# Attention steps of a one-core block laid out anew: values product behind two more products, output parts later, VectorE additions behind the maximum

## What is computed

```
h = rmsnorm(layernorm(x)) * ln_weight
q, k, v = h @ w_q.T, ctx @ w_k.T, ctx @ w_v.T          # 512 -> 32 heads x 128
p = softmax(where(mask, q @ k.T + position_bias, -inf))
x = x + layernorm(x) + (p @ v) @ w_out.T
```

## Time and profile before

| | us |
|---|---|
| runs | 1034.56, 1049.08, 1047.72 |
| median of the runs | 1047.72 |
| the profiled execution | 1043.91 |
| its span, first to last instruction | 1041.8 |

### The profile page before, as it was taken

The page is one execution under the profiler, slowest core; times in us unless marked ns, Lnnn a source line. Parts: engine busy times, 40 slices in busy tenths (PEclk is TensorE's granted clock), DMA queues, the critical chain, the costliest instruction groups (busy, mean ns, idle before and its releaser), DMA issues.

```text
span 1041.8 us, 17308 instructions
## 1 busy us (share of the span) xinstructions
PE 936.6 (90%) x5261; PEld 792.8 (76%) x5261; DVE 721.3 (69%) x1289; ACT 606.9 (58%) x1847; POOL 523.3 (50%) x582
## 2 busy tenths in 40 slices
PE   9989999998988898979898898888897988889998
PEld 8778888886877777867787687777786777668885
DVE  5676965756677586757675667668675868747787
ACT  5777665555656456655564556646565555534564
POOL 2541634574546454654555454645475452204477
PEclk9999999999999999999999999999999999989999
DMA  9223448535565275635672556437562555230101
GB/s 331 68 88 120 162 163 302 206 115 212 184 239 178 95 263 182 236 121 201 206 267 85 212 194 236 149 115 263 179 232 108 204 185 177 88 112 0 32 21 61
DMA packets 61291, 171.70 MB, mean 165 GB/s; under 512 B 6055, under 2 KB 8491, under 8 KB 60988
## 3 DMA queue, kind: packets, MB, share of 16 engines
q1 hardware_dynamic: 61244, 171.11, 47.2%
HBM read 159.56 MB, written 11.53 MB: 164 GB/s over the span
## 4 chain that ended last, share of the span: by engine, by line
PE 53%; DVE 19%; ACT 11%; issue 11%; POOL 4%; DVEq 1%; DMA 1%; SPq 0%; ACTq 0%; POOLq 0%
PE ps_k L363 4%; ACT probs_t L799 4%; PE ps_k L364 4%; PE ps_k L365 4%; PE ps_s L2175 4%; ACT scores L787 4%; PE ps_t L2196 4%; PE ps_o L363 4%; PE ps_q L363 3%; DVE scores L1608 3%; PE ps_q L365 3%; PE ps_v L363 3%; PE ps_q L364 3%; PE ps_v L365 3%; PE ps_v L364 3%
## 5 line engine op out<-in xcount | busy, mean ns | idle before, releaser
L799 ACT COPY probs_t<-scores 32x128 f32<-32x128 f32 x768 | 227.4, 296 | 143.3 <-DVE scores L1612 134.2
L363 PE MATMUL ps_o<-wo_hi,att_hi 128*128 128x512 f32 x256 | 109.0, 426 | 72.5 <-DVE acc L1485 51.8
L787 ACT ACTIVATE scores<-scores,neg_max 128x128 f32<-128x128 f32 x256 | 99.7, 391 | 53.2 <-DVE neg_max L1599 53.0
L363 PEld LDWEIGHTS ps_o<-wo_hi,att_hi 128*128 128x128 f32 x256 | 48.8, 190 | 101.0 <-DVE acc L1485 51.1
L1485 DVE TENSOR_TENSOR acc<-ps_o,acc 128x512 f32<-128x512 f32 x128 | 85.9, 671 | 57.0 <-PE ps_o L365 57.0
L781 ACT CAST att_hi<-ps_t 128x512 fp32r<-128x512 f32 x64 | 37.5, 587 | 146.7 <-PE ps_t L2196 146.6
L1160 POOL TENSOR_TENSOR wq_lo<-raw_q,wq_hi 128x256 fp32r<-128x256 f32 x65 | 47.8, 735 | 125.5 <-ACT wq_hi L620 125.5
L364 PE MATMUL ps_o<-wo_lo,att_hi 128*128 128x512 f32 x256 | 101.9, 398 | 0.0
L365 PE MATMUL ps_o<-wo_hi,att_lo 128*128 128x512 f32 x256 | 101.5, 397 | 0.0
L1119 POOL TENSOR_TENSOR shift<-bias_sb,mask_sb 128x512 f32<-128x512 f32 x64 | 84.5, 1323 | 1.5 <-DVE scores L1595 1.5
L363 PE MATMUL ps_v<-wv_hi,ct_hi 128*128 128x256 f32 x264 | 74.8, 283 | 1.5 <-DVE vv L1439 1.5
(11 more groups left out here) (394 smaller groups left out, 2824.7 us busy)
## 6 DMA issues: line engine op xcount, KB each, us to landing
ring_hi<-scratch_x_t SPq DMA_DIRECT2D x39, 512.0 KB, 4.0
ring_lo<-scratch_x_t SPq DMA_DIRECT2D x39, 512.0 KB, 4.9
ring_hi<-scratch_c_t SPq DMA_DIRECT2D x39, 512.0 KB, 4.2
ring_lo<-scratch_c_t SPq DMA_DIRECT2D x39, 512.0 KB, 5.2
raw_o<-in_w_o SPq DMA_DIRECT2D x16, 512.0 KB, 3.7
raw_q<-in_w_q SPq DMA_DIRECT2D x15, 512.0 KB, 6.1
raw_k<-in_w_k SPq DMA_DIRECT2D x15, 512.0 KB, 7.0
xt_hi<-scratch_x_t SPq DMA_DIRECT2D x13, 512.0 KB, 8.2
```

The costliest lines, as they stand in the source:

```text
L363: pe.matmul(dst, hi_l, hi_r, start=first, stop=False)
L787: e = act.activation(probs[n][:, m, :], scores[n][:, m, :], ACT.Exp, bias=neg_max[:, n, m:m + 1], accum_out=row_sum[:, n, m:m + 1])
L799: last = act.copy(block_of(probs_t, j, i), block_of(scores[n], i, j))
```

## The change

The work is the same; the order on PE, DVE and ACT is another. POOL's and SP's lists are not touched. On PE the values product of a step no longer follows the scores at once but comes behind two (in steps 0 and 4 three) more products, each output part comes about one product later, and the v products and k products around them are dealt out anew; `v_p4` gets a wait for its operand block. On DVE the second residual addition of a step moves into the next step, behind its maximum, together with sums of projections, and the transposes become a function of their own (`turn_blocks`), in steps 3 and 7 behind further additions. On ACT the exponentials come ahead of `attention_high`.

```diff
 # ACT, step
-                attention_high(s - 1)
                 if c % 4 == 2 and more:
                     k_first(G)
+                exponentials(s, n)
+                if c == 4 and coming:
+                    v_first(i + 1, 0)
+                if c % 4 == 1 and more:
+                    q_first(G)
+                attention_high(s - 1)
                 if c % 4 == 3 and more:
                     high_fourth(G)
-                exponentials(s, n)
...
 # DVE, step
                 softmax_front(s, n)
-                attention_rest(s - 1)
+
+                if c == 0 and own:
+                    v_u3(i, 1)
+                if c == 1 and own:
+                    v_c22(i, 1)
+                    v_u4(i, 1)
...
+                add_output(s - 2, (c - 2) % LOOP_STEPS, (1,))
...
+                if c == 3 and own:
+                    v_c21(i, 0)
                 if last and c == 5:
                     q_c12(g)
+                attention_rest(s - 1)
+
+                if c == 7:
+                    k_c11(G)
+                if c == 3:
+                    q_c21(G)
                 softmax_back(s, n)
-                add_output(s - 1, (c - 1) % LOOP_STEPS, (0,))
+                if c % 4 == 3:
+                    add_output(s - 1, (c - 1) % LOOP_STEPS, (0,))
+                    if c == 7:
+                        k_u3(G)
+                        q_c21(G)
+                    k_c21(G)
+                turn_blocks(s, n)
                 if c == 0 and own:
                     v_c22(i, 0)
                     v_u4(i, 0)
...
+                if c % 4 != 3:
+                    add_output(s - 1, (c - 1) % LOOP_STEPS, (0,))
...
-                add_output(s - 1, (c - 1) % LOOP_STEPS, (1,))
...
 # PE, step
                 step_scores(s, c)
+
+                if c % 4 == 0:
+                    q_p5(g)
+                    k_p5(g)
+                if c == 0:
+                    q_p3(g)
+                if c == 4 and coming:
+                    v_p1(i + 1, 0)
+                if c % 4 == 1 and more:
+                    q_p1(G)
+                    q_p6(G)
...
+                if c % 4 == 3:
+                    q_p4(G)
+
                 if c == 0:
                     step_values(s - 1, 7, v_count(i - 1, 14))
...
+                if c == 0:
+                    v_p5(i, 0)
                     k_p3(g)
...
+                    k_p4(G)
                 if c == 4:
                     if coming:
                         v_p1(i + 1, 1)
+                        q_p3(g)
...
+                if c == 7:
+                    k_p2(G)
+                output(s - 1, (c - 1) % LOOP_STEPS, g if c % 4 == 1 else None, (0,))
+
+                if c == 0:
+                    v_p5(i, 1)
+                if c % 4 == 1 and more:
+                    k_p6(G)
...
+                if c == 5 and coming:
+                    v_p6(i + 1, 0)
+                if c == 6:
+                    v_p7(i + 1, 0)
+                if c == 7:
+                    k_p4(G)
...
+                output(s - 1, (c - 1) % LOOP_STEPS, None, (1,))
```

More of the change, by code:

```diff
@@ L857, in step @@
                 if c == 4 and coming:
-                    v_first(i + 1, 0)
                     high_v2(i + 1)
+                    v_first(i + 1, 1)
                 if c % 4 == 0 and more:
                     high_first(G)
-                if c % 4 == 1 and more:
-                    q_first(G)
                 if c % 4 == 2 and more:
@@ L930, in _ @@
             wq1_high_part(3)
-            attention_high(STEPS - 3)
             def mm_high(m):
@@ L1680, in step @@
                 coming = not last
[L1681 to L1688, removed]
+                if c % 4 == 1 and summed and not (last and c == 5):
+                    q_c12(g)
+                if c == 3:
+                    k_c11(G)
+                if c == 6 and coming:
+                    v_u2(i + 1, 0)
+                if c == 7 and coming:
+                    v_u3(i + 1, 0)
+                softmax_front(s, n)
+                if c == 0 and own:
[3 more added lines that the diff above has]
+                    v_u4(i, 1)
                 if c == 4 and not last:
@@ L1706, in step @@
                     q_u4(g)
+                if c % 4 == 1 and summed and not (last and c == 5):
+                    k_c12(g)
+                if c % 4 == 2:
+                    k_u2(G)
+                if c == 6 and coming:
+                    v_u2(i + 1, 1)
                 if c % 4 == 3:
                     q_u3(G)
+                if c == 3:
                     k_u3(G)
[L1710 to L1714, removed]
                 if not own:
@@ L1735, in step @@
                         v_evac(14, 3, 0, done=13)
+                if c % 4 == 2:
+                    q_c11(G)
                 if c == 2 and own:
                     v_c12(i, 1)
-                if c == 3 and own:
-                    v_c21(i, 0)
                 if last and c == 4:
                     v_c21(i, 1)
[L1742 to L1747, removed]
                 if c % 4 == 0 and summed:
@@ L1750, in step @@
                     k_u4(g)
+                if c % 4 == 1 and more:
+                    q_u2(G)
                 if isinstance(i, int) and s == FIRST:
                     block_low(1, wide[0], 7)
[L1753 to L1760, removed]
-                add_output(s - 1, (c - 1) % LOOP_STEPS, (1,))
                 if last and c == 5:
-                    wq1_rest(2)
+                    k_c12(g)
+                    for m in range(3):
+                        wq1_rest(m)
             def target_experts():
@@ L2405, in step @@
                 step_scores(s, c)
+                if c % 4 == 0:
[8 more added lines that the diff above has]
+                    q_p6(G)
+                if last and c == 5:
+                    q_p3(g)
+                if c == 6:
+                    v_p6(i + 1, 1)
+                if c % 4 == 2:
+                    q_p7(G)
+                if c == 2:
+                    q_p2(G)
+                if c == 7:
+                    v_p7(i + 1, 1)
+                if c % 4 == 3:
+                    q_p4(G)
                 if c == 0:
@@ L2498, in step @@
                     v_p4(i, 1)
+                if c == 4 and coming:
+                    v_p2(i + 1, 0)
+                    k_p3(g)
+                if c == 5 and coming:
+                    v_p6(i + 1, 0)
+                if c == 6:
+                    v_p7(i + 1, 0)
+                if c == 7:
+                    k_p4(G)
+                if last and c == 5:
+                    pe.wait_ge(v_out, v_count(i, 14))
+                    for _ in range(4):
+                        pe.matmul(ps_v[:, 0:P], ones[:], ones[:], start=True, stop=True)
+                output(s - 1, (c - 1) % LOOP_STEPS, None, (1,))
+                if c == 1 and not own:
+                    step_v(15, 13, PLAIN)
             for c in range(1, LOOP_STEPS):
```

126 lines of the change are left out of this document (40 added, 86 removed).

## The result

The changed kernel takes 1109.44 us in the median (1109.07 to 1109.97), the kernel before 1047.97: a ratio of 1.062 (95% interval 1.055 to 1.069). The profiled execution's span grew from 1041.8 to 1107.7 us. So it is slower, as forecast, but by 61 us where 25 were forecast, and above the range of 1036 to 1100. (The kernel before has one run more here than in the table of its runs.)

The account below looks back on a forecast made before the run. PE sets the pace, so its waits count. From the profiled 1043.9 us: six turns of +3.45 (+20.7), steps ahead -3, clock +13 less 2, making 1073; range 1036 to 1100, likeliest case 1056 to 1090.

Parts of the forecast that it names:

- forecast, without the clock: Lengths of steps 0 to 7 of the new turn, summing to 115.8 us, +3.45 a turn, before any clock loss.
- The waits for weights: PE waits of 4 to 5 us for `wv_lo` once each in steps 3, 5 and 6, some 80 us or more.
- the third that was named: Over the whole span, PE's waits for `acc` and `att_lo` were to shrink to a third.
- The meetings of DVE and POOL: DVE operations held up by POOL, each meeting costing a whole POOL instruction: 1.1 us in step 6, 1.7 in step 5.
- I take one fall in two: Half of 18 PE waits bring the clock to half, 1.46 us each: +13 us, less 2.
- rival D: The clock falls behind every long wait: 18 x 1.46 = 26 us in place of 13, time 1086; chance 0.18.
- the price of 1.46: Loss in us per clock fall on PE: half of the 2.93 us that PE was busy at half clock.
- less 2 for the three falls that go: Deduction of 2 us from the clock term for the old loop's three falls.
- The unrolled turns on either side share half of their steps with it each: Unrolled turns around the five-turn loop count together as one more turn: six times 3.45 is +20.7 us.
- the steps ahead lose two or three waits: -3: Steps ahead of the loop lose two or three waits for probabilities, 1.2 us each: -3 us.
- Rivals B and C: B: DVE never held up by POOL, 1002 us, chance 0.14; C: gain and loss balance, 1032 to 1057, chance 0.30.

Follow-up runs that it names:

- the run with the weights of step 3 alone: Changed kernel with only step 3's v product weights made sooner, by high_fourth ahead of the exponentials on ACT and v_p4's low part ahead of low_fourth on POOL: 1075.3 us.

## Why the prediction was right in kind and too small

By its own steps, with the turn of the windows above and the run with idle products, in whose loop the clock stays at 1.00:

| step of a turn | forecast, without the clock | changed kernel | with idle products |
|---|---|---|---|
| 0 | 15.4 | 17.23 | 15.74 |
| 1 | 13.8 | 13.30 | 13.98 |
| 2 | 11.7 | 11.99 | 11.95 |
| 3 | 15.6 | 16.70 | 15.53 |
| 4 | 15.0 | 15.60 | 15.62 |
| 5 | 17.4 | 17.95 | 16.66 |
| 6 | 16.3 | 18.36 | 16.23 |
| 7 | 10.6 | 11.20 | 10.78 |
| sum | 115.8 | 122.33 | 116.49 |

- **The waits for weights: right.** PE waits for `wv_lo` in steps 3, 5 and 6, as foreseen, 4.7, 3.4 and 4.2 long. The 80.7 us over the span look like the "some 80 us or more" of the forecast, but 11.0 of them are those of step 1, and step 5's wait is 1.2 shorter than forecast; `acc` and `att_lo` shrank below the third that was named. The ready times were 8.0 in step 3 (forecast 8.3), 13.7 in step 5 (14.6) and 13.1 to 13.5 in step 6 (13.5), and the turn without the clock came out 0.7 us from the forecast. Some luck is in that: single steps are off by up to 0.7 either way, and the errors cancel. Step 3 lies in its range of 15 to 16 without the clock (15.53) and above it with the clock (16.70). The wait of 2.0 in step 0 and that of step 1 were in the sum as well.
- **The meetings of DVE and POOL: right in kind, a little high.** 1.7 was counted in step 5 and 1.1 in step 6. In step 6 the product took 1.19 where undisturbed it takes 0.69, and `row_fac` 0.30 for 0.16, so 0.6; in step 5 the negative maximum took 1.19 for 0.17 and `row_fac` 0.39 for 0.16, so 1.25. These meetings cost what was left of POOL's instruction and not a whole one: in step 5 the maximum began at 462.81, and POOL's instruction of 2.40 us ended at 463.96. The forecast for step 5 was 0.9 late, in part for this reason.
- **Failed: "I take one fall in two".** The 18 waits for weights in steps 3, 5 and 6 came with half clock 18 times out of 18, so rival D had the mechanism, though 1086 is still short of 1109. Four of the six waits of 2.0 in step 0 came with it as well, which neither the forecast nor D had: 22 falls in place of 9. As the run with idle products shows, the clock is worth at least 1107.7 - 1079.0 = 28.7 us of span; the forecast had 11. That is some 1.3 us for each of the 22, so the price of 1.46 was near and the count failed. That the price was near is luck: by the pace of the matmuls some 45% of the work at half clock is lost and not half, and four of the 18 windows are 6.83 long, which makes 69.6 us of work in all and a loss of about 1.7 each, of which the next wait takes a part back. And "less 2 for the three falls that go" does not agree with 1.46 each, which is 4.4.
- **Failed: the turns outside the loop.** "The unrolled turns on either side share half of their steps with it each" gave them 3.45 together, and "the steps ahead lose two or three waits: -3". By the stages above, steps 8 to 15 grew by 6.3 and the last turn by 12.1, and the steps ahead by 1.3. With idle products it is still 5.5, 9.9 and 2.0. The first of the two has the waits of steps 5 and 6 just as the loop has (3.4 and 4.1). In the last, PE waits 4.6 in step 3 for weights, and 3.3 and 2.2 in steps 4 and 5, where the next turn's v products are missing, so that nothing stands between output parts any more. I had read the waits of the loop and not the order of these fourteen steps.

The sum: 65.9 us of span were added and 28.7 forecast. Of the 37.2 that are missing, the clock has 17.7, the unrolled turns 12 (15.4 with idle products against 3.45, and in that the three windows at half clock that are left there), the steps ahead 5 and the loop's waits 2.7 (19.9 against 17.25). Rivals B and C are out with their conditions: step 5 is not below 16, nor a turn below 115.

The Trainium skill (TensorE: Matmul & The Clock Gate, "HAM oscillation") would have been the better guide here than the three falls in the loop of the kernel before, as it says that idle stretches between bursts bring the clock down each time. The trace agrees for the waits of 3.4 us and more (18 of 18), and in part for that of 2.0 (4 of 6). It is no law for single waits: in the run with the weights of step 3 alone, two of the six waits of 3.4 in step 5 left the clock at 1.00.

## What to carry to other kernels

Who moves a product to an earlier place must move what makes its operands, on every engine of the chain, in the same edit: here seven moves on ACT and POOL turned a loss of 6% into a gain of 4%, with PE's order unchanged. A longer wait of TensorE is to be counted with the half clock that may come with it. Here 22 waits of 2.0 to 4.7 us, 82 us in all, cost some 29 us of span in that way, a third of their own length again; which waits do, the trace of the same kernel has to show. And steps written out ahead of and behind a loop are to be walked through by themselves, above all those in which the filling work is missing.

## What was not expected of the hardware

Stretches at half clock came in two lengths, 3.41 and 6.83 us, in the loop the longer with the waits of 3.4 and 4.2 us in steps 5 and 6 in some turns and not in others. The same wait of 2.0 in step 0 brought the clock down in four turns of six; why just these was not tried. Matmuls that nobody reads, run through a wait, kept the clock of the loop at 1.00 and were worth 30.5 us, while a product that they stand ahead of started at the same place (`v_p4(i, 0)` 8.1 us behind the scores, 8.0 without them). And of a meeting of DVE and POOL either side can bear the cost: one cost DVE 1.05 us (1.74 for 0.69), the other POOL 0.53 (1.82 for 1.29), and 0.1 us of a start stood between them.
